# The tail of expert tiles in a graph layer with a routed feed-forward: transposes three tiles ahead, three output banks, one expert number per load

## What is computed

```python
def _L0_gnn_ref(X, A, Wv, bv, aw, ab, Wk, bk):
    ...
    alpha_matrix = A * jnp.exp(e)
    transition = alpha_matrix / (jnp.sum(alpha_matrix, axis=-1, keepdims=True) + 1e-12)
    ...
    return jax.nn.relu(H)

def _L0_ffn_ref(x, switch_w, switch_b, expert_w, expert_b):
    ...
    routes = jnp.argmax(probs, axis=-1)
    oh = jax.nn.one_hot(routes, E, dtype=jnp.int32)
    pos = jnp.take_along_axis(jnp.cumsum(oh, axis=0), routes[:, None], axis=1)[:, 0] - 1
    capacity = int(CAPACITY_FACTOR * N / E)
    keep = pos < capacity
    buf = jnp.zeros((E, capacity, D), dtype=xf.dtype).at[routes, pos].set(xf)
    y = jnp.einsum('ecd,efd->ecf', buf, expert_w) + expert_b[:, None, :]
    gathered = y[routes, jnp.minimum(pos, capacity - 1)]
    out = jnp.where(keep[:, None], gathered, xf) * route_probs[:, None]
    return out.reshape(B, S, D)
x = x + _L0_gnn_ref(_layernorm(x, axis=-1), adj, ...)
x = x + _L0_ffn_ref(_layernorm(x, axis=-1), ...)
```

## Time and profile before

| | us |
|---|---|
| median of 3 runs | 755.63 |
| lowest, highest | 754.70, 755.71 |
| profiled execution | 753.94 |
| its span, first to last instruction | 752.2 |
| PE, PEld busy | 713.5, 632.3 |
| DVE, ACT, POOL busy | 641.0, 479.5, 444.8 |

### The profile page before, as it was taken

The page is one execution under the profiler, slowest core; times in us unless marked ns, Lnnn a source line. Parts: engine busy times, 40 slices in busy tenths (PEclk is TensorE's granted clock), DMA queues, the critical chain, the costliest instruction groups (busy, mean ns, idle before and its releaser), DMA issues.

```text
span 752.2 us, 18567 instructions
## 1 busy us (share of the span) xinstructions
PE 713.5 (95%) x4857; PEld 632.3 (84%) x4857; DVE 641.0 (85%) x3101; ACT 479.5 (64%) x1508; POOL 444.8 (59%) x526
## 2 busy tenths in 40 slices
PE   8999999999999999999999999999999999958873
PEld 7788887889999998999898999999999989847762
DVE  6899999998988998999889899889998888776553
ACT  3567776766676666666666666666676676544541
POOL 4435554456666666766656666676666665665563
PEclk9999999999999999999999999999999999999998
DMA  9623544444444334445434433444443323244430
GB/s 279 174 77 105 161 147 134 142 134 135 135 154 136 116 129 154 155 143 156 140 129 148 146 115 116 147 150 144 144 144 115 123 81 100 95 150 142 124 102 0
DMA packets 93001, 100.12 MB, mean 133 GB/s; under 512 B 10395, under 2 KB 85208, under 8 KB 92898
## 3 DMA queue, kind: packets, MB, share of 16 engines
q1 hardware_dynamic: 77012, 65.96, 29.5%
q0 software_dynamic: 13008, 30.07, 10.9%
q10 hardware_dynamic: 2880, 2.92, 1.4%
HBM read 49.92 MB, written 54.72 MB: 139 GB/s over the span
## 4 chain that ended last, share of the span: by engine, by line
PE 86%; DVE 8%; issue 2%; POOL 1%; another core or an unknown queue 1%; ACT 0%; POOLq 0%; DVEq 0%
PE ps_z12a L1320 11%; PE ps_z12b L1320 11%; PE ps_lgb L1320 9%; PE ps_z0a L1320 8%; PE ps_z0b L1320 7%; PE ps_lga L1435 5%; PE ps_z0a L1403 4%; PE ps_z0b L1403 4%; PE ps_z12b L1382 4%; PE ps_xt L1422 3%; PE ps_xt L1350 3%; PE ps_z12a L1382 3%; PE ps_lgb L1464 3%; PE ps_t L1396 2%; PE ps_t L1371 2%
## 5 line engine op out<-in xcount | busy, mean ns | idle before, releaser
L555 POOL DMA_INDIRECT out<-lent,tok x143 | 145.5, 1018 | 158.4 <-DVE lent L1236 136.1
L542 POOL DMA_INDIRECT rowbuf<-rows,idx x128 | 129.7, 1013 | 54.4 <-issue 30.3
L620 ACT CAST xth<-ps_xt 128x256 fp32r<-128x256 f32 x128 | 47.7, 373 | 112.9 <-PE ps_xt L1350 110.7
L497 POOL TENSOR_SCALAR x<-xin,nm,r 128x256 f32<-128x256 f32 x128 | 84.5, 661 | 24.7 <-PE ps_xt L1350 18.8
L695 ACT ACTIVATE x<-rin 128x256 f32<-128x256 f32 x143 | 86.9, 608 | 3.1 <-issue 1.6
L1435 PEld LDWEIGHTS ps_lga<-swc,xft 128*128 128x128 f32 x512 | 76.4, 190 | 10.7
L677 ACT ACTIVATE od<-rows,oc,oa 128x256 f32<-128x256 f32 x128 | 77.1, 602 | 0.1
L835 DVE TENSOR_TENSOR xtl<-ps_xt,xth 128x256 fp32r<-128x256 f32 x128 | 53.9, 421 | 16.5 <-ACT xft L669 16.3
L493 POOL TENSOR_TENSOR r<-ve,mhalf 128x4 f32<-128x4 f32 x31 | 32.2, 1039 | 56.9 <-ACT ve L655 56.4
L1435 PE MATMUL ps_lga<-swc,xft 128*128 128x16 f32 x512 | 65.6, 241 | 0.0
L641 ACT ACTIVATE e<-ps_t,svs 128x128 f32<-128x128 f32 x128 | 47.0, 367 | 17.6 <-PE ps_t L1396 15.1
(11 more groups left out here) (215 smaller groups left out, 2393.0 us busy)
## 6 DMA issues: line engine op xcount, KB each, us to landing
rin<-rowbuf SPq DMA_DIRECT2D x143, 130.0 KB
out<-od SPq DMA_DIRECT2D x32, 512.0 KB
xin<-in_x SPq DMA_DIRECT2D x31, 512.0 KB, 4.1
ain<-in_adj SPq DMA_DIRECT2D x32, 256.0 KB, 4.5
ewr<-in_ewT SPq DMA_DIRECT2D x16, 256.0 KB, 2.6
out<-lent,tok POOLq DMA_INDIRECT x143
rowbuf<-rin ACTq DMA_DIRECT2D x1, 2080.0 KB, 13.5
rowbuf<-rows,idx POOLq DMA_INDIRECT x128
```

The source lines that it names most:

```text
L497: pool.tensor_scalar(x0[:, g % 2, :], xin[:, g % BODY, :], nm1[:, q, g % G:g % G + 1], r1[:, q, g % G:g % G + 1], ALU.add, ALU.mult).then_ ...
L542: pool.indirect_dma_start(out=rowbuf, out_offset=bass.IndirectOffsetOnAxis(ap=idx[:, i:i + 1], axis=0), in_=rows[:, r, :], in_offset=None, ...
L555: pool.indirect_dma_start(out=out.rearrange("g n d -> (g n) d"), out_offset=bass.IndirectOffsetOnAxis(ap=tok[:, i % RY:i % RY + 1], axis=0 ...
```

## The change

Transposes have four banks: the free `ps_xt` joins, and `high(i)` and `low(i)` read bank i mod 4 (`rows_bank`). Sums have three: `ps_z0b`, `ps_z0a` and `ps_log` (shown as `ps_lga`) in turn from tile 97 (`out_of`). Behind the products of tile i, from tile 98 on, TensorE transposes tile i+3; ScalarE's and VectorE's orders move along: `high(i+2)`, `norm(i+4)` and `low(i+2)`, `finish(i)`. The products wait for the finish of tile i-3. The two new banks were in use until the last logits, so the transposes of tile 100 wait for `s_xfe`, the products of tile 99 for `s_lgr`.

Expert numbers are loaded one by one: that of tile i+1 behind the first product of tile i. VectorE bounds each table entry by `TOP` with an instruction of its own (`tile_bounds`; in `last_tiles` it is part of one that was there), and SyncE's check of each entry at run time goes. `tile_experts`, which signals `s_tab`, stands one place later.

```diff
-        ps_bx = [*ps_z12, ps_tile]
-        ps_by = ps_z0
+        ps_bx = [ps_xt, ps_z12[1], ps_tile, ps_z12[0]]
+        ps_by = [ps_z0[1], ps_z0[0], ps_log]
...
+        def rows_bank(i):
+
+            return ps_tile if i < WOVEN else ps_bx[i % 4]
+
+        def out_of(i):
+
+            return ps_tile[:, D:2 * D] if i < WOVEN else ps_by[(i - WOVEN) % 3][:, 0:D]
...
-                    tab_row[0:1, i:i + m], [mybir.EngineType.SP], min_val=0, max_val=TOP)
+                    tab_row[0:1, i:i + m], [mybir.EngineType.SP], min_val=0, max_val=TOP,
+                    skip_runtime_bounds_check_because="VectorE takes each entry's minimum with TOP")
...
             def tile(i):
-                if i + 1 < NT:
-                    high(i + 1)
-                if i + 3 < NT:
-                    norm(i + 3)
+                if i + 2 < NT:
+                    high(i + 2)
+                if i + 4 < NT:
+                    norm(i + 4)
...
             norm(WOVEN + 4)
+            high(WOVEN + 3)
+            default_rows(IT, G30 + 2)
+            norm(WOVEN + 5)
             for i in range(WOVEN + 2, NT):
-                tile(i)
-                g = G30 + 2 + i - WOVEN - 2
+                g = G30 + 3 + i - WOVEN - 2
                 if g < BODY:
                     default_rows(IT, g)
+                tile(i)
...
                 if names is not None:
-                    tile_experts(names)
+                    tile_bounds(names)
...
                 if names is not None:
+                    tile_experts(names)
                     reached(names)
...
+            def tile_bounds(c):
+                after(c, 9)
+                i = (c - FIRST_STEP) * G
+                dve.tensor_scalar(tab_row[:, i:i + G], tab_row[:, i:i + G], TOP, None, ALU.min).then_inc(s_pick, 1)
...
-                    link(15, dve.tensor_tensor(tab_row[:, STEPPED:NT], base[:], stop[:], ALU.min))
+                    link(15, dve.scalar_tensor_tensor(tab_row[:, STEPPED:NT], base[:], float(TOP), stop[:], ALU.min, ALU.min))
...
             def tile(i):
-                if i + 1 < NT:
-                    low(i + 1)
+                if i + 2 < NT:
+                    low(i + 2)
                 finish(i)
...
             last_step(NG - 1)
+            low(WOVEN + 3)
             for i in range(WOVEN + 2, NT):
...
                 if i < WOVEN:
                     ge(pe, b_fin, i)
                 else:
-                    pe.wait_ge(b_lo, i - 2)
+                    pe.wait_ge(b_lo, i - 3)
                 if i == WOVEN:
                     pe.wait_ge(s_z1, B)
-                if WOVEN <= i < WOVEN + 3 and i % 3 == 2:
+                if i == WOVEN + 1:
                     pe.wait_ge(b_fin, WOVEN)
+                if i == WOVEN + 3:
+                    pe.wait_ge(s_xfe, B)
...
-                if i >= WOVEN + 2:
-                    pe.wait_ge(b_fin, i - 1)
+                if i == WOVEN + 2:
+                    pe.wait_ge(s_lgr, NG)
+                if i >= WOVEN + 3:
+                    pe.wait_ge(b_fin, i - 2)
...
                 for part, t in PARTS:
+                    if WOVEN - 1 <= i < NT - 1 and i + 1 not in at and (part, t) == PARTS[1]:
+                        experts_of(i + 1, 1)
...
             def tile(i):
                 expert(i)
-                if i + 1 < STEPPED and (i + 1) % G == 0:
-                    experts_of(i + 1, G)
-                if i + 1 >= STEPPED and (i + 1 - STEPPED) % LOADED == 0:
-                    experts_of(i + 1, min(LOADED, NT - i - 1))
-                if i + 2 < NT:
+                if i <= WOVEN + 1:
                     turn(i + 2)
+                if i > WOVEN and i + 3 < NT:
+                    turn(i + 3)
```

More of the change, by code:

```diff
@@ L35 @@
 LAG_TILE = 16
-LOADED = 4
 def graph_then_experts(nc, x, adj, WvT, bv, aw, ab, Wk, bk, swT, sb_, ewT, eb, out):
@@ L699, in high @@
                 act.wait_ge(b_xt, i + 1)
-                src = ps_tile if i < WOVEN else ps_bx[i % 3]
-                act.copy(xth[:, xr(i), :], src[:, 0:D]).then_inc(b_hi, 1)
+                act.copy(xth[:, xr(i), :], rows_bank(i)[:, 0:D]).then_inc(b_hi, 1)
             def tile(i):
-                if i + 1 < NT:
-                    high(i + 1)
-                if i + 3 < NT:
-                    norm(i + 3)
+                if i + 2 < NT:
+                    high(i + 2)
+                if i + 4 < NT:
+                    norm(i + 4)
             def first_moments(lo, signal):
@@ L1089, in row_of_token @@
                                          ALU.add).then_inc(s_slot, 1)
-            NPK = 12
+            NPK = 13
             def by_tile(v, n):
@@ L1148, in tile_rows @@
                     dve.tensor_reduce(tab_row[:, i:i + G], pick[:, 0:G, :], AX_X, ALU.add).then_inc(s_pick, 1)
+            def tile_bounds(c):
+                after(c, 9)
+                i = (c - FIRST_STEP) * G
+                dve.tensor_scalar(tab_row[:, i:i + G], tab_row[:, i:i + G], TOP, None, ALU.min).then_inc(s_pick, 1)
             def tile_experts(c):
-                after(c, 9)
+                after(c, 10)
                 i = (c - FIRST_STEP) * G
@@ L1164, in advanced @@
             def advanced(c):
-                after(c, 11)
+                after(c, 12)
                 dve.tensor_tensor(done[:], want[:], have[:], ALU.min).then_inc(s_pick, 1)
@@ L1178, in last_step @@
                 tile_rows(c)
+                tile_bounds(c)
                 tile_experts(c)
@@ L1220, in low @@
                 dve.wait_ge(b_hi, i + 1)
-                src = ps_tile if i < WOVEN else ps_bx[i % 3]
-                dve.tensor_tensor(xtl[:, xr(i), :], src[:, 0:D], xth[:, xr(i), :].bitcast(F32),
+                dve.tensor_tensor(xtl[:, xr(i), :], rows_bank(i)[:, 0:D], xth[:, xr(i), :].bitcast(F32),
                                   ALU.subtract).then_inc(b_lo, 1)
@@ L1227, in finish @@
                 c, r = i % RY, i % RI
-                src = ps_tile[:, D:2 * D] if i < WOVEN else ps_by[i % 2][:, 0:D]
+                src = out_of(i)
                 dve.wait_ge(b_y, i + 1)
@@ L1284, in _ @@
             candidates(IT, G31)
+            tile_bounds(c)
+            first_candidate(IT, G31)
             tile_experts(c)
-            first_candidate(IT, G31)
             reached(c)
@@ L1455, in turn @@
                 else:
-                    pe.wait_ge(b_lo, i - 2)
+                    pe.wait_ge(b_lo, i - 3)
                 if i == WOVEN:
                     pe.wait_ge(s_z1, B)
-                if WOVEN <= i < WOVEN + 3 and i % 3 == 2:
+                if i == WOVEN + 1:
                     pe.wait_ge(b_fin, WOVEN)
+                if i == WOVEN + 3:
+                    pe.wait_ge(s_xfe, B)
                 pe.wait_ge(b_xf, i + 1)
-                dst = ps_tile if i < WOVEN else ps_bx[i % 3]
+                dst = rows_bank(i)
                 for t in range(KT):
@@ L1488, in expert @@
                 pe.wait_ge(b_lo, i + 1)
-                y = ps_tile[:, D:2 * D] if i < WOVEN else ps_by[i % 2][:, 0:D]
+                y = out_of(i)
                 c = xr(i)
                 for part, t in PARTS:
+                    if WOVEN - 1 <= i < NT - 1 and i + 1 not in at and (part, t) == PARTS[1]:
+                        experts_of(i + 1, 1)
                     ts = slice(t * P, (t + 1) * P)
```

## The result

| | before | after |
|---|---|---|
| median of 10 runs each, us | 755.50 | 752.28 |
| lowest, highest | 754.14, 757.51 | 751.82, 754.64 |
| profiled execution, its span | 753.94, 752.2 | 752.48, 750.7 |
| scatter of tile 96 | 660.16 | 658.72 |
| scatters of tiles 104 and 142 | 681.44, 743.24 | 680.07, 741.78 |

The ratio of the medians is 0.9963, with a 95% interval from 0.9955 to 0.9972: the change is worth 0.37%, some 2.8 us (the medians lie 3.2 apart). The forecast was 6.3 us. Its sign and its full range (742 to 754.5) held, the band of its own mechanism (745.5 to 752) did not; the size is nearest to that of the second rival, "held notices win" (753.5).

The account below looks back on a forecast made before the run. The latency of the ring TensorE, ScalarE, VectorE, TensorE was taken as the bound, with two tiles of lead. Less 4.9 (lead), less 2.0 (start), plus 0.2 (loads), plus 0.4 (minimum): 755.63 - 6.3 = 749.3 us, range 742 to 754.5.

Parts of the forecast that it names:

- band of its own mechanism: Whole kernel: the forecast's own case, 749.3 us, from 745.5 to 752, chance 0.54.
- second rival: Tail: holes stay whole or grow with the burst, 1.59 us a tile or worse; 753.5 us, chance 0.25.
- the ring with late notices: Tail: latency of TensorE, ScalarE, VectorE, TensorE bounds it, two tiles of lead covering notices up to 1.8 us late.
- Lead of three: Steady tail, tiles 104 to 142: 1.63 to 1.50 us a tile, 4.9 us saved, bounds 1.5 and 13.1.
- poor end: Steady tail: rounds of four tiles with the hole whole, 1.59 us a tile, 1.5 us saved.
- SyncE's checks: SyncE's row loads: two fewer sequencer instructions a tile, worth nothing in the steady tail, counting only at its start.
- Start of the tail: Tiles 100 to 104: VectorE's 3.16 us wait shrinks, 2.0 us saved (0 to 3.2).
- Register loads: TensorE from tile 100 on: 32 more loads, 0.2 us lost on the path (0 to 10.6).
- third rival: Tail: exposed register loads become TensorE's bound, 1.84 us a tile, 8.0 us lost, 762 us; chance 0.08.
- VectorE's minimum: Table steps: one more instruction each, 0 in the woven part, 0.4 us lost between its end and tile 100.

Follow-up runs that it names:

- no_scatters_2: The changed kernel without the scatters of tiles 102 to 142, on a chip of 755: 727.98 us, one run.
- paced_long: The changed kernel with one larger GpSimd write behind each scatter of the tail, scatters 1.51 us apart: 751.04 us, 0.9946 of the kernel before.
- after_fours: The changed kernel with the tail's expert numbers loaded four at a time between two tiles: 751.33 us, 0.9955 of the kernel before.
- lead_alone_2: The kernel before with the lead of three tiles, four banks and three, keeping SyncE's checks and loads of four: 753.03 us, 0.9970 of before.
- checks_alone_2: The kernel before without SyncE's checks and with VectorE's minimum, on a chip of 755: 753.25 us, 0.9979 of before.
- before_again: The kernel before, word for word, profiled a second time on a chip of 755: 754.9 to 755.5 us over its two profiles.
- checks_alone: The kernel before without SyncE's checks and with VectorE's minimum, on a chip of 735: 735.01 us, 0.9997 of before.
- loads_alone_2: The kernel before with the tail's expert numbers loaded singly, lead of two and checks kept, on a chip of 755: 756.07 us, 1.0012 of before.
- empty_scatters: The changed kernel with the scatters of tiles 102 to 142 bounds-checked at row 0, hardly a row written, on a chip of 735: 735.61 us, before 735.31.

## Why the prediction was right or wrong

**What bounds the kernel.** Right on this chip, and now shown: the ring with late notices. "What holds the notices back, the trace doesn't say": the scatters do, by no_scatters_2, and their spacing sets how long a hole follows, by paced_long. That it was a property of the kernel and not of the chip that it was profiled on was taken for granted and is false.

**Lead of three, 4.9 us.** This is the term that failed. The lead gained 2.3 us in all (ratio 0.9970; 1.4 to 3.0 us), and in the steady tail about 1.8 of the 4.9: 60.3 and 60.7 us where the kernel without it takes 61.7, 61.8 and 63.5. The step that was wrong is the choice inside the bounds: "one more tile of lead the ring should look everywhere as it does there", in the stretch of the earlier trace rows with 1.51 a tile. That stretch begins behind one hole and ends in front of the next. The scatter that follows it, tile 123's in the kernel before, stands behind a hole of 1.31:

```profile
713.21 0.98 POOL L555 DMA_INDIRECT out<-lent,tok  x1 [1.31 <-DVE lent L1236]
```

With it the stretch is six steps in 713.21 - 703.35 = 9.86 us, 1.64 each, no better than the tail's 1.63. So the 1.51 was a round without its hole and not a faster ring. I also took the spaced scatters in it (1.28 to 1.92 us apart) for the effect of a ring that keeps up; paced_long shows that spacing works as a cause too: forced to 1.51, it gives 58.80 / 38 = 1.55 a tile. A third tile of lead does the opposite, it makes longer bursts, with longer holes behind them. The poor end of the same sum, a round of four with the whole hole, 1.59, is what after_fours (60.33 / 38 = 1.588) and lead_alone_2 (1.597) measured.

**SyncE's checks, 0.** Right in the steady tail (61.73 us in checks_alone_2, at the lower of the two of before, 61.80), wrong in all: 1.6 us [0.9 to 2.3] for the checks with the minimum that replaces them, at the finish of tile 95, in the last woven slots, where the step had looked only at the tail's start.

**Start of the tail, 2.0 us.** Wrong, it gave next to nothing. From the scatter of tile 97 to that of 104 the kernel before takes 681.44 - 662.25 = 19.19 us, the changed one 680.07 - 660.80 = 19.27, lead_alone_2 19.21. Two other profiles without the lead have 19.60 (before_again) and 19.52 (checks_alone_2), so 0.4 at most. VectorE's longest wait there is 1.78 now and no longer 3.16, and the time is lost elsewhere: ScalarE has the transposed rows late again.

```profile
670.82 0.37 ACT L708 CAST xth<-ps_z12a 128x256 fp32r<-128x256 f32 x1 [2.15 <-PE ps_xt L1484]
```

These rows were ready at 667.99 by TensorE's timeline (667.36 + 0.63). The windows of the changed kernel also show the granted clock at 0.50, the lower level of 1.2 GHz, through 665 to 670, behind a stretch in which TensorE worked 3.21 of 5 us; before, it was 0.66 in the same window.

```profile
660.00:665.00 5.00, 3.21 (x13) 2.49 (x13) 4.21 (x27) 4.86 (x11) 3.29 (x4) 0.65 0.32 112
665.00:670.00 5.00, 4.66 (x20) 4.38 (x21) 3.35 (x14) 1.17 (x3) 3.77 (x5) 0.50 0.76 227
```

But the clock is no difference that counts: in the same window it was 0.50 in before_again too, and in checks_alone on the chip of 735, where the stretch takes 15.47 us and not 19.

**Register loads, 0.2 us.** Too small: 0.9 us by loads_alone_2 [0.3 to 1.6], and the same by the medians of the changed kernel and after_fours, whose intervals overlap. The loads themselves are as short as forecast, 310 ns in the median (row below), but the gap from first to second product is 0.48, above the 0.4 that was named as the mark. By the floor of about 600 ns that the prediction quoted from the Trainium skill ("DMA: Bandwidth & Descriptors", Latency and other measured facts) they would be twice as long; 310 ns decides. The step that failed is "under a tail in which it idles over 1 us in a round": TensorE idles because its input is late, and when it restarts, its own time is on the path, 0.15 us more a tile and 0.36 more in the tile that restarts it. The prediction named that tile and put too little on it. The third rival's direction was right, not its size: it would have needed 0.56 us exposed. (Its 762 is counted from the profiled execution; from the median, as the other times are, the same 8.0 us make 763.6.)

```profile
L1491 PEldq TENSOR_LOAD <-tab_exp x68: 296/310/574, 152.9 to 735.4; - x68
```

**VectorE's minimum, 0.4.** Not visible in the woven part, as forecast: from the finish of tile 0 to that of tile 94 the kernel before takes 488.47 us, the changed one 488.26. In the tail it was not measured alone; no run shows the 0.4.

**The sum.** Forecast 4.9 + 2.0 - 0.2 - 0.4 = 6.3. Measured 2.3 (lead) + 0 (start, which is in the lead's 2.3) + 1.6 (checks) - 0.9 (loads) = 3.0. The second rival came nearest in time, 753.5, and had the mechanism, but not all of the parts: it put the start at 1.0 and the checks at nothing. That the forecast's full range held is partly luck: the lead with the start gave 4.6 us less than forecast, and 1.6 came from a term that was put at nothing.

## What to carry to other kernels

More lead hides a delay that is there whatever one does; it hides little of one that grows with the work that the lead lets through. Before a pace from a good stretch of a trace is taken as the target, count whole rounds, with the hole in them, and ask whether the good stretch is the cause or the effect. And take a register load out of the middle of a tile's products unless that engine has slack on the path: here, with a lead of two, loads of four between two tiles are better by 0.9 us on one kind of chip and by 4.6 on the other.

## What the runs showed of the hardware

While GpSimd issues indirect DMAs 0.30 us apart, TensorE's notices reach ScalarE and VectorE up to 2.8 us late on one kind of chip (755 us for the kernel before) and 0.04 us after the end on another (735 us). With 0.44 us between the scatters the holes in the tail stay; with 0.53 all but two or three of them vanish, though the notices are still late (2.2 us in the round shown for paced_long). Without scatters they come 0.04 us after the end (no_scatters_2). The woven part is the same on both (488 us from the finish of tile 0 to that of 94); of the 17.5 us between the spans of the kernel before (752.2) and of checks_alone on the other kind (734.7), 12.6 are in the last 38 steps (61.80 against 49.23) and 3.7 between the scatters of tiles 97 and 104 (19.19 against 15.47). The Trainium skill ("Perfetto Trace Analysis", DMA Instruction — SWDGE (GPSIMD)) says that the end shown for such a DMA is the end of GpSimd's descriptor generation and not of the transfer; the rows here fit that, 0.98 us shown for each scatter while the nearly empty ones of empty_scatters landed 2.5 us behind their issue (its DMA view of 690 to 740 us: count, median us to landing).

```profile
out<-lent,tok POOLq DMA_INDIRECT x28, 2.5
```

Whether the descriptors or the rows that move hold the notices, and what differs between the chips, stays open: the run that was to tell the first fell on the chip that has no late notices.
